# Score matmuls of two streams issued in turn, the second stream's pairs of head groups in the other order

## The reference, cut to what matters

```
scores = q @ k.T / sqrt(8)        # (64, 64), then the mask, if there is one
attn   = softmax(scores)
ctx    = attn @ v                 # (64, 8)
```

## Time and profile before

| | |
|---|---|
| median of 3 runs | 1410.59 us (1410.39 to 1410.71) |
| span of the profiled execution | 1411.3 us |
| PE busy / instructions | 1225.6 us (87%) / 9592 |
| DVE busy | 614.8 us (44%) |
| ACT busy | 513.9 us (36%) |
| POOL busy | 337.2 us (24%) |

### The profile page before, as it was taken

One profiled execution on the slowest core, in us unless ns is written; L12 is line 12 of the kernel. 1 busy time (PEld: TensorE's weight loads), 2 busy tenths in 40 slices (PEclk: granted clock), 3 DMA queues, 4 the chain that ended last, 5 costly groups with the idle time before them and its releaser, 6 DMA issues. The chain is left out here.

```text
span 1411.3 us, 24787 instructions
## 1 busy us (share of the span) xinstructions
PE 1225.6 (87%) x9592; PEld 934.4 (66%) x9592; DVE 614.8 (44%) x1438; ACT 513.9 (36%) x1219; POOL 337.2 (24%) x312
## 2 busy tenths in 40 slices
PE   5898889888879998888897888988799989899894
PEld 4566666666657778777566777856577756766662
DVE  3434544445434336463444556454333334344332
ACT  3332434335335552323241232333244443244251
POOL 1011025020240514411203421220422361230412
PEclk9688778898779997879777788977699987778797
DMA  9000000000051231000000000000022130000022
GB/s 340 4 1 1 2 1 29 18 1 1 1 163 58 80 119 66 12 1 1 0 2 3 23 21 1 0 1 1 18 67 77 54 120 5 1 31 1 26 81 68
DMA packets 54033, 52.93 MB, mean 38 GB/s; under 512 B 6816, under 2 KB 49312, under 8 KB 53024
## 3 DMA queue, kind: packets, MB, share of 16 engines
q1 hardware_dynamic: 48800, 40.85, 8.9%
q0 software_dynamic: 5120, 10.50, 2.5%
HBM read 34.02 MB, written 17.30 MB: 36 GB/s over the span
## 5 line engine op out<-in xcount | busy, mean ns | idle before, releaser
L361 POOL TENSOR_TENSOR small<-small,neghalf 128x4 f32<-128x4 f32 x56 | 56.7, 1020 | 612.9 <-DVE small L383 414.9
L639 DVE TENSOR_REDUCE mx<-bank 128x8 f32<-128x512 f32 x128 | 88.1, 688 | 170.8 <-PE bank L478 144.4
L568 ACT ACTIVATE probsT<-bank 128x512 f32<-128x512 f32 x128 | 73.9, 597 | 195.3 <-PE bank L490 195.3
L1537 PEld LDWEIGHTS bank<-wmoe,otx 128*128 128x128 f32 x764 | 103.1, 191 | 51.7 <-issue 40.2
L1226 POOL DMA_INDIRECT yg<-ybuf,posi x80 | 77.1, 963 | 218.8 <-DMA ybuf<-otx 191.7
L501 PEld LDWEIGHTS bank<-vblk,probsT 128*64 128x64 f32 x2048 | 86.5, 165 | 51.3 <-issue 32.6
L501 PE MATMUL bank<-vblk,probsT 128*64 128x18 f32 x2048 | 98.5, 233 | 18.4 <-DVE upd L627 16.3
L490 PE MATMUL bank<-csb,probs 128*128 128x128 f32 x512 | 102.1, 345 | 13.3 <-ACT probs L572 13.3
L1537 PE MATMUL bank<-wmoe,otx 128*128 x764 | 105.9, 276 | 4.2 <-DVE otx L1639 1.8
L286 PE MATMUL bank<-warm_x,warm_w 128*128 128x224 bf16 x540 | 104.5, 300 | 0.0
L490 PEld LDWEIGHTS bank<-csb,probs 128*128 128x128 f32 x512 | 75.1, 177 | 40.3 <-issue 20.9
(11 more groups left out here) (271 smaller groups left out, 2184.6 us busy)
## 6 DMA issues: line engine op xcount, KB each, us to landing
ybuf<-otx SPq DMA_DIRECT2D x122, 64.0 KB
xblk<-xbuf SPq DMA_DIRECT2D x26, 256.0 KB
wmoe<-in_w_moe SPq DMA_DIRECT2D x3, 2048.0 KB, 10.1
wmoe<-in_w_moe SPq DMA_DIRECT2D x1, 3072.0 KB, 10.4
xbuf<-otx SPq DMA_DIRECT2D x2, 1472.0 KB, 19.9
wmoe<-in_w_moe SPq DMA_DIRECT2D x1, 1536.0 KB, 13.8
xbuf<-rows,posi POOLq DMA_INDIRECT x80, 2.2
yg<-ybuf,posi POOLq DMA_INDIRECT x80
```

Source lines behind the costliest of these rows:

```text
L639: link(c, dve.tensor_reduce(s.mx[:, k % 2, :], s3, AX.X, ALU.max))
L1537: mm = pe.matmul(YB[:, 0:P], aT[:, na % 3, ch * P:(ch + 1) * P], wmoe[:, bass.ds(e * (H * P) + at, P)], start=(ch == 0), stop=(ch == H - 1))
```

## The change

The second stream's `scores` takes the pairs of head groups in the other order (`first = 64 * pair ^ 32 * s.turned`, where `turned` is 0 or 2: rows 64 to 127 first in stream 1, then 0 to 63), and its `weigh` writes the unit's result to the group that the unit now holds. `scores` is cut into three slots: masks, four matmuls, four matmuls, so that masks of both streams come first and then four matmuls of each in turn. A unit has 5 slots instead of 3 on all engines; where there is nothing for the two new ones they are empty. `catch_up` gives two empty slots to pair 2 (stream 0) after its first norm, on PE, ACT, DVE and POOL, in all three lanes. No arithmetic is added or removed.

```
--- before.py
+++ after.py
@@ Stream.__init__
+                self.turned = 2 * i
@@ heads_pe, scores(tile, pair), behind the waits and the masks
-                for i, g, b2 in np.ndindex(2, 2, 2):
-                    r = slice(64 * pair + 32 * g, 64 * pair + 32 * g + 32)
-                    b = BT * tile + 2 * i + b2
-                    mm = pe.matmul((SA, SB)[g][b2 * SEQ:(b2 + 1) * SEQ, i * T:(i + 1) * T],
-                                   qT[r, b * SEQ:(b + 1) * SEQ], s.k4[r, :, b, :], start=mask is None, stop=True,
-                                   skip_group_check=True)
-                    if i == 1 and b2 == 1:
-                        mm.then_inc(*c.give("scores"))
+                yield
+                first = 64 * pair ^ 32 * s.turned
+                for i in range(2):
+                    for g, b2 in np.ndindex(2, 2):
+                        r = slice(first + 32 * g, first + 32 * g + 32)
+                        b = BT * tile + 2 * i + b2
+                        mm = pe.matmul((SA, SB)[g][b2 * SEQ:(b2 + 1) * SEQ, i * T:(i + 1) * T],
+                                       qT[r, b * SEQ:(b + 1) * SEQ], s.k4[r, :, b, :], start=mask is None, stop=True,
+                                       skip_group_check=True)
+                        if i == 1 and b2 == 1:
+                            mm.then_inc(*c.give("scores"))
+                    yield
@@ heads_pe, weigh(k)
-                tile, g = divmod(k, 4)
+                tile, g = k // 4, k % 4 ^ s.turned
...
-                if g == 3:
+                if k % 4 == 3:
                     mm.then_inc(*c.give("context"))
@@ heads_pe, the units
                 if k % 2 == 0 and k < UNITS:
-                    scores(k // 4, k // 2 % 2)
-                yield
+                    yield from scores(k // 4, k // 2 % 2)
+                else:
+                    yield from idle(3)
@@ heads_pool
-            yield from idle(3 * (UNITS + 1) + 2)
+            yield from idle(5 * (UNITS + 1) + 2)
@@ heads_dve, each unit
+                yield from idle(2)
@@ new
+        def catch_up(p):
+
+            yield from idle(PREP if p == 2 else 0)
@@ a1, a2, a3 on pe, act, dve and pool, behind the first norm
+            yield from catch_up(p)
```

## The result

The changed kernel takes 1340.4 us (median of four runs, 1338.2 to 1349.3) against 1410.5 for the kernel before on the same chip: a ratio of 0.954 (0.950 to 0.959), 70 us less. The forecast was 1397.6 with a range of 1380 to 1424. The direction was right, the size was not: the time lies 40 us under the range. Medians here are of all runs of a kernel, and ratios with their intervals leave out a run that is over 1.5% above the fastest of its kernel. A second run of the changed kernel on another chip gave 1342.7 against 1408.6, ratio 0.956 (0.952 to 0.959).

What follows compares the result with a forecast made beforehand. TensorE, busy 87% of the span at a clock moving between 1.2 and 2.4 GHz, was taken as the bound. 1411.3 - 27 (heads) + 14 (catch-up) = 1398.3 profiled, so 1397.6 us measured; range 1380 to 1424.

Steps and rivals of the forecast that it cites:

- The overlap of two row-group pairs: Score matmuls: both streams' calls on different row groups overlap fully; a masked pair takes 2.03 us instead of 3.12.
- rival 2: Score calls: streams don't overlap, only masks and drains are saved; +10 to +25 us, about 1427; chance 0.10.
- The chain behind it: Softmax after merged scores: two reduces of 0.69 us follow back to back, shrinking the gain where TensorE waits (k=0, k=4).
- some 10: Sign: TensorE's waits for the first exponential and the normed context grow together by some 10 us.
- The catch-up at 14 us: Second halves of layers: holding stream 0 back two slots makes them like the slower first halves, costing 14 us.
- the bounds of 0 and 28.7: Catch-up's cost in us: nothing, or the full difference between first and second halves of the layers.
- the heads' 27 us: Eight head phases with both streams: merged score calls save 27 us in all, ends 18 and 36.
- The pairs at k=2 and k=6: Score calls in a full queue, mostly at half clock: each masked pair gains 1.55 us, between 1.1 and 2.0.
- Layer 1's first stretch: Sign: layer 1's first half, from stream 1's projection to its `prep`, gets shorter by about 7 us.
- rival 3: Whole span: clock rises, fewer slow stretches, catch-up costs nothing; gain 27 to 36 us, about 1380; chance 0.18.

Runs made afterwards that it cites:

- e5: Changed kernel with each stream's eight score matmuls in one piece, stream 0's then stream 1's, instead of four in turn: 1340.8 us, ratio 0.957.
- e2: Kernel before with only the catch-up added (no turned order, three-slot units, scores in one piece): 1423.2 us against 1407.5, ratio 1.015.
- e9: Changed kernel with each stream's eight score matmuls in one piece and the catch-up empty: 1388.2 us against 1399.5 for the kernel before.
- e1: Changed kernel with the catch-up empty, so stream 1 is two slots behind in pairs 2 and 3: 1400.8 us against 1407.5, ratio 0.998.
- e6: Changed kernel with five unread 32-row matmuls behind each stream's last four in 24 of 32 merged calls: 1382.0 us, kernel before 1403.5.
- e4: Changed kernel with five unread 128-row matmuls behind each stream's last four in 24 of 32 merged calls: 1363.7 us, kernel before 1403.5.
- e13: Kernel before with 8 unread matmuls for each stream in two TensorE waits of each head phase: 1340.0 us against 1408.6, ratio 0.953.
- e8: Kernel before with five unread matmuls instead of three for each unit of a head phase: 1377.3 us against 1403.5, ratio 0.983.
- e14: Changed kernel with score calls of eight in one piece, catch-up empty and both head-phase waits filled with unread matmuls: 1349.8 us, ratio 0.959.

## Why the prediction was wrong, by its own steps

- **The overlap of two row-group pairs** was right: eight tiles at once, 2.01 us for a masked pair of calls where 2.03 was worked out, L482's busy time 45.4 where "near 50" was said. The Trainium skill's rule that matmuls start and end strictly in program order ("TensorE: Matmul & The Clock Gate", section "The mechanism") would have made rival 2; the measurement differs: in e5 stream 1's eight matmuls stand behind all of stream 0's, and its first four start before stream 0's last four, 32 records in 0.77 us.
- **The chain behind it** was right in kind and in sum: two reduces back to back (1.42 us at 1101.00), waits for the exponential from 13.3 to 22.9 us and for the normed context from 16.3 to 17.0, together 10.3 where "some 10" was said. That the sum fits is luck: each of the two was charged 0.69 a phase, and over eight phases the first grew by 1.2 each and the second by 0.1.
- **The catch-up at 14 us** was near as a price of its own: e2 measured 16 beside the kernel before, in a wide interval. In the changed kernel the second halves do look like the first, as forecast (153.0 and 152.7, 205.9 and 211.3, 72.7 and 71.7 us). The first halves won 47.2 us and the second 22.5, so by an estimate (the heads win the same in both halves) level order still costs about 25, within the bounds of 0 and 28.7. What the prediction missed is that the changed kernel can't do without it: leaving it out costs some 48 to 60 us (e9, e1). It took the longer units to cost nothing in both orders. A slip beside it: of the 28.7 us, 1.8 are layer 2's, so not all are in layers 1 and 3.
- **The term that failed is the heads' 27 us.** It should have been 84 with the catch-up at its 14, or 94 if the first halves' 47.2 counts for both and the catch-up is 25. The pairs at k=2 and k=6 were priced at 1.55, between 1.1 (slow time lasts as before) and 2.0 (the clock is what it was), and both bounds had the slow stretches stay. Over the whole run they did not stay: 466 us at the low level became 341. In the second cycle of layer 3, 12.69 us at 0.67 became 7.87 at 1.00, 4.8 us for one pair. Layer 1's first stretch was to be some 7 us shorter and is 26.1. That was rival 3, put at 1380 and at 18 in 100; its first half, the rising clock, was right and its size too small (that the catch-up costs nothing was not), because I priced there only the absence of a cost, not the slow time that comes back as full-clock time: 466 us of it before, a third of the span, and half of each microsecond of it was to be had. The rows for this stood in the prediction, for time by clock was seen to be equal in stretches of the same work. It was read as a price of the catch-up only, and not as what a denser queue in the head phases could win.

How the clock follows from the order is not settled. The clock was lower with sparse fillers than with dense ones (e6 against e4), and filled waits raised it most for the matmuls they take (e13 against e8). Which of the two the merged calls did more of is open: they shorten sparse time and also lengthen waits, and I know of no run that separates these without changing both.

## What to carry to other kernels

Where the engine that bounds the kernel spends a third of the span at the low clock, price an edit by slow stretches that may vanish or appear, not only by its microseconds: multiply each stretch by its mean clock; nearly equal products for the same work say that the clock is what differs. Try the cheap test first: unread dense matmuls in the engine's longest waits. Here they gave as much as the overlap, and what the overlap is worth at a high clock (12 to 16 us) was seen only beside them. When two streams are to meet in the same slot, hold them level, for here longer units together with the lag that suited the short ones gave a lower clock (e9, e14).

## What the runs showed of the hardware

- Tiles on four row groups and two column groups run together: the 32 records of a merged call start within 0.75 us at full clock, where the 16 of a single call took 0.72. A matmul on free row groups need not wait for those ahead of it in the queue: in e5 stream 1's first four start within 0.07 us of stream 0's first, and four of stream 0's that stand ahead of them start 0.48 us after it.
- Nearly the same work ran at very different mean clocks: layer 1's first stretch at 0.79 before, 0.92 after, 0.96 with filled waits. Few matmuls change it: 8 for each stream in two waits of a phase (e13).
- Ten unread matmuls a call on 32 rows instead of 128, for nearly the same time, leave the clock at 0.863 to 0.869 instead of 0.874 to 0.880 (e6, e4).
